# A post-norm transformer layer on one core: GpSimd's long operations and the first norm's statistics take other places in a hand-written order

## The reference

```python
def _layernorm(x, axis=-1, eps=1e-05):
    m = jnp.mean(x, axis=axis, keepdims=True)
    v = jnp.var(x, axis=axis, keepdims=True)
    return (x - m) / jnp.sqrt(v + eps)
...
q = query @ wq + query @ Aq @ Bq * LORA_SCALE
k = query @ wk
v = query @ wv + query @ Av @ Bv * LORA_SCALE
q = apply_rope(q, sin, cos)
k = apply_rope(k, sin, cos)
scores = jnp.einsum('bhqd,bhkd->bhqk', q, k) / jnp.sqrt(jnp.float32(dh))
scores = jnp.where(causal[None, None], jnp.float32(-1000000000.0), scores)
attn = jax.nn.softmax(scores, axis=-1)
out = jnp.einsum('bhqk,bhkd->bhqd', attn, v)
return out @ wo                      # after merging the heads
...
h = butterfly(x @ W_exp + b_exp, up_weights)
h = butterfly(gelu(h + up_bias), down_weights)
y = h @ W_con + b_con + down_bias
...
x = _layernorm(x + attention(x))
x = _layernorm(x + ffn(x))
```

## Time and profile before

| what | value |
|---|---|
| median of the runs | 1245.32 us |
| profiled execution, its own time | 1246.34 us |
| its span, first to last instruction | 1244.6 us |
| TensorE matmuls busy | 1127.5 us, 91% |
| VectorE busy | 872.7 us, 70% |
| ScalarE busy | 674.8 us, 54% |
| GpSimd busy | 494.8 us, 40% |
| mean granted TensorE clock | 0.932 |

### The profile page before, as it was taken

The page is one execution under the profiler, slowest core; times in us unless marked ns, Lnnn a source line. Parts: engine busy times, 40 slices in busy tenths (PEclk is TensorE's granted clock), DMA queues, the critical chain, the costliest instruction groups (busy, mean ns, idle before and its releaser), DMA issues.

```text
span 1244.6 us, 27684 instructions
## 1 busy us (share of the span) xinstructions
PE 1127.5 (91%) x8462; PEld 819.2 (66%) x8462; DVE 872.7 (70%) x1951; ACT 674.8 (54%) x1067; POOL 494.8 (40%) x539
## 2 busy tenths in 40 slices
PE   4777799999999999999999999999999999989876
PEld 3555467676676767666676767667676766767565
DVE  6589866777767677786767677776767777676432
ACT  2167565574745566474646547464555647455601
POOL 5333426263443526253342626343352634423301
PEclk8678799999998989899898989999898999989989
DMA  7673545555463536545363655546255553632111
GB/s 260 146 210 93 175 95 189 122 167 140 127 179 94 180 96 199 127 138 154 95 198 69 204 121 156 144 98 206 65 191 120 181 135 114 180 86 73 60 38 34
DMA packets 94983, 169.90 MB, mean 137 GB/s; under 512 B 14872, under 2 KB 36120, under 8 KB 94944
## 3 DMA queue, kind: packets, MB, share of 16 engines
q1 hardware_dynamic: 93888, 166.53, 48.4%
q10 hardware_dynamic: 832, 1.83, 0.4%
q0 software_dynamic: 224, 1.04, 0.2%
HBM read 92.28 MB, written 77.07 MB: 136 GB/s over the span
## 4 chain that ended last, share of the span: by engine, by line
PE 68%; DVE 19%; issue 6%; DMA 3%; ACT 2%; POOL 1%; DVEq 1%; SPq 0%; POOLq 0%; ACTq 0%
PE ps_m L560 23%; PE ps_m L709 17%; PE ps_m L679 7%; PE ps_m L608 7%; PE ps_t L651 5%; PE ps_m L688 5%; DVE x_res L974 4%; DVE m_raw L905 4%; DVE m_raw L900 3%; PE ps_m L637 2%; PE ps_m L694 2%; DVE stats L959 1%; DVE rope_in L923 1%; DVE m_pad L914 1%; DVE rope_in L924 1%
## 5 line engine op out<-in xcount | busy, mean ns | idle before, releaser
L781 ACT ACTIVATE pT<-ps_t 128x512 f32<-128x512 f32 x640 | 330.2, 603 | 230.3 <-PE ps_t L651 229.9
L1046 POOL TENSOR_SCALAR_AFFINE_SELECT pT<-pT 128x512 f32<-128x512 f32 (+1 forms) x320 | 179.3, 561 | 546.4 <-ACT pT L781 545.0
L905 DVE TENSOR_REDUCE m_raw<-ps_m 128x1 f32<-128x512 f32 (+2 forms) x768 | 339.0, 503 | 70.9 <-PE ps_m L637 67.3
L709 PE MATMUL ps_m<-w,gact 128*128 128x256 f32 x1024 | 231.6, 382 | 1.1 <-ACT gact L851 1.1
L709 PEld LDWEIGHTS ps_m<-w,gact 128*128 128x128 f32 x1024 | 191.9, 190 | 29.7 <-ACT gact L851 1.5
L608 PE MATMUL ps_m<-k_st,q_st 48*128 48x512 f32 (+3 forms) x1024 | 157.1, 363 | 44.0 <-DMA k_st<-qk_scr 15.0
L608 PEld LDWEIGHTS ps_m<-k_st,q_st 48*128 48x128 f32 x1024 | 92.0, 196 | 108.2 <-issue 83.1
L679 PE MATMUL ps_m<-pT,v_aug 128*32 128x512 f32 (+3 forms) x2048 | 157.7, 450 | 2.0 <-POOL pT L1046 1.4
L651 PE MATMUL ps_t<-q_st,k_st 50*128 50x512 f32 (+3 forms) x1024 | 128.9, 360 | 5.5 <-DMA q_st<-m_scr 3.7
L952 DVE TENSOR_TENSOR y<-ps_m,y 128x256 f32<-128x256 f32 x64 | 27.2, 425 | 143.9 <-PE ps_m L709 143.9
L679 PEld LDWEIGHTS ps_m<-pT,v_aug 128*32 128x32 f32 x2048 | 59.1, 112 | 85.9 <-issue 77.6
(11 more groups left out here) (106 smaller groups left out, 1664.5 us busy)
## 6 DMA issues: line engine op xcount, KB each, us to landing
qk_scr<-rot_hi SPq DMA_DIRECT2D x64, 512.0 KB, 3.6
q_st<-qk_scr SPq DMA_DIRECT2D x128, 192.0 KB, 4.6
k_st<-qk_scr SPq DMA_DIRECT2D x128, 192.0 KB, 5.0
qk_scr<-rot SPq DMA_DIRECT2D x32, 512.0 KB, 4.1
o_scr<-o_raw SPq DMA_DIRECT2D x64, 256.0 KB, 2.2
r_b<-in_xT SPq DMA_DIRECT2D x17, 512.0 KB, 6.2
o_c<-o_scr SPq DMA_DIRECT2D x32, 256.0 KB
r_b<-r_scr SPq DMA_DIRECT2D x32, 256.0 KB
```

The lines of the kernel that those rows point to most:

```text
L709: mm = pe.matmul(pm[:, 0:D], gact[:, k, n * P:(n + 1) * P], w2[:, k, :], start=(k == 0), stop=(k == NHT - 1))
L781: act.activation(pT[:, g % 2, slot, half * T:(half + 1) * T], ps_t[:, ST_BANK[2 * n + r], :], ACT.Exp, scale=SCALE).then_inc(exp_done, 1)
L905: ins = dve.tensor_reduce(m_raw[:, r, u // 2, qt:qt + 1], scores[:, off:off + (qt + 1) * P], AX.X, ALU.max, negate=True)
L1046: pool.affine_select(out=v, in_=v, compare_op=ALU.is_ge, fill=0.0, base=0, pattern=pattern, channel_multiplier=-1).then_inc(mask_done, 1)
```

## The change

No instruction is added, taken away or altered; only places in `steps` differ. With the diff's own names: `ON` of the first half goes from the end of phase 0 to the end of phase 2; `BIAS` of both halves, from the end of phase 0 into phases 1 and 3; `XRES` of the second half from phase 1 to phase 3; `XLO` behind the masks of phase 7; the first statistics `LNS` between the two `WO` adds; the aggregation `LNA` behind the transposition of the maxima in phase 6. The order of TensorE and ScalarE is the same as before.

```diff
@@ early, p == 1
             put("MROW", i, 1)
+            put("BIAS", i - 2, 0)
@@ early, p == 3
             put("RB", i - 1, 1)
+            put("BIAS", i - 2, 1)
+            put("XRES", i - 1, 1)
@@ early, p == 5
             gemm("WO", i - 1, 0)
+            put("LNS", i - 1, 0)
             gemm("WO", i - 1, 1)
@@ early, p == 6
             gemm("MT", i, 3)
+            put("LNA", i - 1, 0)
             put("MROW", i, 3)
@@ late
         elif p == 1:
             put("XRES", i - 1, 0)
-            put("XRES", i - 1, 1)
...
         elif p == 5:
-            put("LNS", i - 1, 0)
             put("LNS", i - 1, 1)
...
         elif p == 7:
             put("LNS", i - 2, 3)
-            put("XLO", i + 2, 0, B + 1)
             put("FILL", i + 1, 2)
@@ last
-        if p == 0:
+        if p == 2:
             put("ON", i - 1, 0)
-            put("BIAS", i - 2, 0)
-            put("BIAS", i - 2, 1)
-        elif p == 5:
-            put("LNA", i - 1, 0)
+        elif p == 7:
+            put("XLO", i + 2, 0, B + 1)
```

## The result

The kernel does not get faster. The changed kernel takes 1252.68 us, the median of six runs (1248.88 to 1255.27); the kernel before, run beside it, takes 1243.16. The ratio is 1.0067, with a 95% interval of 1.0043 to 1.0092: slower by 0.7%, where 1175 us were forecast. The profiled execution took 1248.88 us, with a span of 1247.1.

The account below looks back on a forecast made before the run. TensorE was taken as the bound, with idle time and clock to win: 38.4 us from 13 periods, 29.3 from the clock, some 2.5 elsewhere, together 70.2, from 1246.3 to 1176.1, 1175 against the runs; own range 1169 to 1187, widened 1168 to 1206.

Parts of the forecast that it names:

- The bound: Whole period: TensorE bounds it, busy 68.28 of 71.60 us; only its idle 3.3 us and its clock can be won.
- the stretch: Phases 6 and 7: normalisation beside `XLO` falls from 3.72 to 2.0 us; with the shorter path `XT` starts 2.3 us earlier.
- the clock: Behind `XT`: TensorE's clock stays full once the gaps go, 2.6 us a period, 29.3 us in all.
- rival A: Behind `XT`: all idle time goes as said but the half-clock stretch stays; 1204 us, chance 0.15.
- End of phase 0: End of phase 0: L916 drops from 1.21 to some 0.2 us and TensorE's wait goes; 0.65 us a period, 0 to 0.85.
- `ON`, `SMOC` and `BIAS`: From phase 2 to `WO`: later `ON` delays `SMOC` 4.8 us, 0.4 us left before `WO`; costs nothing, high end 1 us a period.
- The term of `XRES`: Second half's `XRES`, issued behind `RB` some 12 us later, still lands before its first need; cost put at nothing.
- The signs that the prediction had listed for B or C: Reciprocal (L939) beginning later than 494 us in its period's terms, or `WO` waiting for o_c.
- B: Add of phase 3 or `WO`: later `ON` makes a new wait of 1 us a period; 1189 us, chance 0.16.
- C: Reciprocal and add: s_m lands over 7.8 us after issue, holding VectorE, slower than before; 1266 us at 9.3, chance 0.03.
- D: Normalisation: its 2.5 us stay wherever `XLO` stands, as does the low clock; only 17 us won, 1228 us, chance 0.03.

Follow-up runs that it names:

- the vector part alone: The kernel before with only `XLO`, `LNS` and `LNA` moved as in the change, `ON`, `BIAS` and `XRES` at their old places: 1185.81 us, ratio 0.9509.
- both halves of the vector part: Two runs on the kernel before: `XLO` alone moved behind the masks of phase 7, 1189.8 us; `LNS` and `LNA` alone moved, 1184.35 us.

## Why the prediction was wrong

**The bound, the stretch and the clock: right.** Without the late `ON`'s effect the time is 1180 to 1186 us in five kernels (`ON` put back; the vector part alone; `SMOC`'s wait changed, with and without the store on ScalarE's queue; `ON` one phase earlier), against the forecast's 1175, inside its own range of 1169 to 1187. The average period is 66.05 to 66.8 us against 66.1. The normalisation shrank as said, the waits ahead of `XT` and for the copy are gone, and the clock stays at 1.00 when the long gap goes. The sizes came out too. From the first `XT` to the fourteenth, 13 periods, TensorE's idle time is 44.0 us before (923.4 - 879.4) and 8.7 us with `SMOC`'s edit (858.6 - 849.9), 35.2 us less where 38.4 were forecast, and its busy time is 29.6 us less where 29.3 were forecast for the clock. The stated range was narrower than its own terms: for phase 0 it took 0.3 us as the low end where the section says 0, which would make 1191 us and not 1187. The Trainium skill ("TensorE: Matmul & The Clock Gate", section "A second HAM failure mode: psum-queue depth-cycling") had made rival A possible, with its clock that swings because of frequent short pauses between groups of matmuls; the periods at 1.00 throughout, 66.00 and 67.00 us, in kernels that cycle through the same four PSUM banks, speak against it here.

**"End of phase 0", 0.65 us a period: about right.** TensorE's wait for the rotary input, of the kernel with `ON` back in phase 0 and of the one with `SMOC`'s wait changed:

```profile
PE ps_m L608 <- DVE rope_in L924: 11.5, 15, 2.2
```

```profile
PE ps_m L608 <- DVE rope_in L924: 4.4, 3, 2.2
```

These are 7.1 us over 12 periods, 0.6 us in each, and the average period is 66.05 against 66.57 us. The times (1183.03 and 1185.74) differ the same way, but their intervals overlap.

**"`ON`, `SMOC` and `BIAS`", "At nothing, high end 1 us a period": the step that failed.** Its first half came true nearly to the letter. `SMOC` is late by the 4.3 us that SyncE stands for `ON` (4.8 forecast), the reciprocal waits for s_m, and the add behind it has room. VectorE's timeline:

```profile
573.35 0.54 DVE L939 RECIPROCAL r_m<-s_m 64x64 f32<-64x64 f32 x1 [1.55 <-DMA s_m<-o_scr]
574.92 0.42 DVE L952 TENSOR_TENSOR y<-ps_m,y 128x256 f32<-128x256 f32 x1 [1.02 <-PE ps_m L709]
```

The add still waits 1.02 us for TensorE, so no VectorE time is lost there. What went wrong is two things.

First, each transfer was priced by its landing in the old surroundings. `REC` took 2.3 us when it was issued 1.2 us behind two stores of 512 KB; now it is issued 0.3 us behind them. The row of DMA issues from 574 to 575 us:

```profile
r_scr<-r_m SPq DMA_DIRECT2D x1, 16.0 KB, 4.7
```

That is 2.4 us more, r_b's load waits for it, and the 0.4 us that I had left ahead of `WO` became a wait of 1.3 us (16.7 over 13).

Second, and this is the larger part, I wrote that "SyncE's next stores and `REC` stand behind it" and followed the chain only as far as `WO`. The queue does not end there: x_res, `QKL`, the third row of maxima, `FILL` and the input come behind `RB`, and the fourth row of maxima after them. I had named the free time of 4.9 us ahead of that store nowhere, since it was nobody's wait. Now 1.1 us are left of it, the landing takes 5.9 us instead of 2.3, and 2.96 us of that reached TensorE, right behind the place where 1.85 us had been won, and with it the clock. Over all kernels with `FILL` ahead of the store in SyncE's queue the landing grows as this time shrinks, though at 3.6 us the landings still differ by 1.6 us, for a reason that no run shows. Each row is read in one period of that kernel's trace:

| kernel | us from the last load of `FILL` to the store | us to the store's landing |
|---|---|---|
| before | 4.9 | 2.3 |
| before, `XLO` alone moved | 4.9 | 1.8 |
| `ON` put back | 3.6 | 2.6 |
| `SMOC`'s wait changed | 3.6 | 3.1 |
| the vector part alone | 3.6 | 3.4 |
| before, the statistics alone moved | 3.6 | 4.0 |
| `ON` one phase earlier | 3.6 | 4.2 |
| before, `ON` alone moved | 3.3 | 3.6 |
| `BIAS` and `XRES` put back, `ON` late | 1.9 | 5.4 |
| changed | 1.1 | 5.9 |
| changed, `QKH` behind `RB` | 0.5 | 6.5 |

The table also shows that 1.3 of the 3.8 us went with the gain itself: a faster VectorE has the maxima ready sooner, so that the store moves up to the loads (4.9 to 3.6 us). The late `ON` takes the other 2.5 us, and only with that does `ST` wait for 2 to 3 us in each period. This is why the same move costs so much less in the kernel before.

The term of `XRES`, "At nothing", was wrong with it: with `ON` late, `XRES` and `BIAS` in their new places cost 13 us (0.8 us of the free time, by the table); with `ON` early, nothing.

In numbers: the forecast gain was some 70 us. With `SMOC`'s edit 61 us of it are there (1243.91 to 1183.03), and without it the changed kernel gives back 70 us (1252.68 against 1183.03): by the spans 48 us as TensorE's idle time and 21 us as its lower clock.

**The rivals.** The signs that the prediction had listed for B or C were both there: the reciprocal begins 48.2 us after `XT` (573.35 - 525.18), where 494 us stood for 47.7, and `WO` waits for o_c. B named `WO`'s wait and priced it rightly at about 1 us a period, 16 us in all, but it was the small half. C had the outcome and the queue (a chain behind the late `ON`) and gave it 0.03; its mechanism, s_m landing over 7.8 us after its issue and holding back VectorE, is not what happened (the reciprocal starts 2.3 us after s_m's issue, and the add still waits for TensorE). A is what the changed kernel looks like from the clock, but for another reason: a new gap stands in for the old one. D is refuted, by both halves of the vector part.

**What stays open.** Why the clock keeps 1.00 in single periods with the gap (740.60; 305.90 before), in five of eleven with the two old gaps when `ON` alone is moved, and in only the first when `QKH` stands behind `RB`, was not tried. How much of the late store is due to the input's 512 KB was not separated: in the kernel with `FILL` moved the input's load still stands 3.7 us ahead of the store (571.97 to 575.70), about as far as in the changed one (3.5 us), and the store lands in 1.4 us. So the loads of `FILL` are needed for the delay; whether they would do without the input's is not shown.

## What to carry to other kernels

When an operation moves later, follow every in-order queue that has a wait for it, to the end of the period and not to the next consumer, and write down for each small transfer how long the engines had been idle ahead of it: that idle time is a resource that no view lists as a wait. Price a transfer by the row of the surroundings that it moves into. And before moving the operation, look whether the wait on it guards what is really shared; here a wait that was stricter than the buffers needed cost 70 us behind the late `ON`, and a wait for the reciprocal, which guards the same buffer, cost nothing.

## What the runs showed of the hardware

A write of 16 KB to HBM lands in 1.4 us with the DMA engines idle (before, at 499.91 us), in 2.3 us when it is issued 4.9 us behind the last of four loads of 192 KB, with the engines running empty (30% of their share until the landing), in 4.7 us when 0.3 us behind two stores of 512 KB, and in 5.9 us when 1.1 us behind four loads of 192 KB and 3.5 us behind one of 512 KB (79%); issued from ScalarE's queue it takes 5.8 us in the same place.

A VectorE instruction on SBUF that meets a GpSimd operation with two inputs in SBUF stands until that is through: 2.51 us instead of 0.41 for L974 beside `XLO` (2.46 us), 1.21 instead of 0.18 for L916 beside `ON` (1.27 us). Where the two were moved apart, both were short again. Because of that the loss hangs on 0.7 us of relative position, and an edit of VectorE's order alone removed it. The Trainium skill ("GPSIMD Engine Reference", section "8. Key points") says that the two engines share their SBUF interfaces and contend when VectorE's instruction has two SBUF inputs or runs in a two-port mode; L916, with two SBUF inputs, agrees; which mode L974 runs in, no row here shows.

Behind gaps of 0.72 and 1.86 us in a period of 71.6 us TensorE's clock was at 0.50 for 6.8 us in eleven of twelve periods of the kernel before, and in six of eleven when `ON` alone was moved; with the 0.72 us gap alone it stayed at 1.00 in all 13 periods.
